# State-space stage of a two-layer decoder: a table of slots with an order of its own for each engine, and block-step rows in the decay matmul in place of the mask matmul

## The reference

```
xBCzA = input @ in_proj_w.T            # 1536 conv channels, 512 z, 64 heads of dt
xBC   = silu(causal_conv4(xBC) + bias) # x 512 (64 heads x 8), B and C 8 groups x 64
dt    = softplus(A_log);  dA = -dt
# in chunks of 128 tokens, s = query, z = key, for each of 64 heads:
Lm[s,z]    = exp(sum of dA over z < k <= s), 0 for z > s
Y_diag     = (C @ B.T * Lm) @ x
Y_off      = the state of the chunk before, decayed, through C
out        = ((Y_diag + Y_off + D * x / dt) * silu(z + z_bias)) @ out_proj_w.T
```

## Time and profile before

| | us |
|---|---|
| median of 3 timed runs | 995.61 (993.46 to 995.78) |
| the profiled execution | 996.49 |
| its span, first to last instruction | 994.6 |
| first decay slot of stage D to the last | 458.7 to 694.2 |
| TensorE, VectorE, ScalarE, GpSimd busy over the span | 807.5, 584.1, 381.4, 220.8 |
| granted TensorE clock, mean | 0.902 |

### The profile page before, as it was taken

How to read it: one execution, slowest core, us unless ns; L and a number is a source line. 1 busy time by engine, 2 the same in 40 slices (tenths; PEclk the granted TensorE clock), 3 DMA queues, 4 the chain that set the end, 5 groups by cost and what they waited for, 6 DMA issues and landing times.

```text
span 994.6 us, 14755 instructions
## 1 busy us (share of the span) xinstructions
PE 807.5 (81%) x5680; PEld 527.0 (53%) x5680; DVE 584.1 (59%) x1188; ACT 381.4 (38%) x653; POOL 220.8 (22%) x210
## 2 busy tenths in 40 slices
PE   1577777599799799656999898998667786899998
PEld 0334443258577578543444454343445464677776
DVE  5666642544445457635787888568567653545443
ACT  1124334101434345234455555454124344444442
POOL 4200000123442322141110111011311201432432
PEclk9889988799899899866899999699778788799999
DMA  8000001000121221000000000000000001222231
GB/s 311 28 2 1 3 1 49 1 0 21 57 70 62 65 63 33 9 0 5 5 4 5 4 4 6 3 5 4 1 2 2 1 2 50 75 85 64 82 95 41
DMA packets 17831, 32.77 MB, mean 33 GB/s; under 512 B 5819, under 2 KB 9787, under 8 KB 17494
## 3 DMA queue, kind: packets, MB, share of 16 engines
q1 hardware_dynamic: 17762, 31.83, 10.3%
HBM read 29.85 MB, written 1.05 MB: 31 GB/s over the span
## 4 chain that ended last, share of the span: by engine, by line
PE 60%; DVE 20%; issue 10%; ACT 5%; POOL 3%; DMA 1%; SPq 0%; DVEq 0%; ACTq 0%; POOLq 0%
PE bank L1355 13%; PE bank L1379 8%; PE bank L1394 5%; PE bank L1117 3%; PE bank L1455 3%; PE bank L1302 3%; PE bank L1453 3%; DVE s_xn L1526 2%; PE bank L1317 2%; DVE s_arena L1598 2%; PE bank L1246 2%; PE bank L1493 2%; PE bank L1400 2%; PE bank L1189 1%; POOL s_rstd L727 1%
## 5 line engine op out<-in xcount | busy, mean ns | idle before, releaser
L779 POOL TENSOR_TENSOR s_wl<-s_wmoe,s_wh 128x768 fp32r<-128x768 f32 x54 | 99.2, 1839 | 175.8 <-ACT s_wh L949 175.8
L898 ACT ACTIVATE s_arena<-bank 128x512 f32<-128x512 f32 x96 | 56.7, 597 | 107.3 <-PE bank L1222 56.8
L1717 DVE TENSOR_TENSOR s_act<-bank,s_sg_moe 128x512 f32<-128x512 f32 x54 | 37.3, 692 | 83.1 <-PE bank L1355 76.5
L1598 DVE TENSOR_REDUCE s_arena<-bank 128x2 f32<-128x512 f32 (+1 forms) x96 | 64.7, 687 | 34.0 <-PE bank L1193 17.3
L1355 PE MATMUL bank<-s_xh,s_wh 128*128 128x512 f32 x216 | 73.3, 422 | 9.0 <-POOL s_wl L779 9.0
L961 ACT CAST s_ah<-s_act 128x512 fp32r<-128x512 f32 x54 | 33.6, 621 | 102.6 <-DVE s_act L1722 79.3
L1355 PE MATMUL bank<-s_xl,s_wh 128*128 128x512 f32 x216 | 70.2, 408 | 0.0
L1379 PE MATMUL bank<-s_wh,s_ah 128*128 128x256 f32 x216 | 66.4, 308 | 2.8 <-DVE s_al L1728 2.8
L1355 PE MATMUL bank<-s_xh,s_wl 128*128 128x512 f32 x216 | 68.5, 399 | 0.0
L1752 DVE SCALAR_TENSOR_TENSOR s_arena<-s_arena,s_convw 128x256 f32<-128x256 f32 x144 | 67.9, 513 | 0.6
L1818 DVE TENSOR_TENSOR s_arena<-s_arena 128x512 f32<-128x512 f32 x64 | 43.4, 686 | 37.7 <-ACT s_arena L1058 37.5
(11 more groups left out here) (224 smaller groups left out, 1702.6 us busy)
## 6 DMA issues: line engine op xcount, KB each, us to landing
s_wmoe<-in_wF SPq DMA_DIRECT2D x28, 384.0 KB, 3.1
s_wmoe<-in_wC SPq DMA_DIRECT2D x26, 384.0 KB, 3.1
s_win<-in_win SPq DMA_DIRECT2D x1, 2112.0 KB, 10.4
s_x<-in_x SPq DMA_DIRECT2D x4, 256.0 KB, 3.4
s_early<-in_ctxT SPq DMA_DIRECT2D x1, 1024.0 KB, 9.5
s_ctxn<-in_ctx SPq DMA_DIRECT2D x1, 1024.0 KB, 12.2
s_arena<-s_arena SPq DMA_DIRECT2D x64, 6.0 KB
out_x<-s_x SPq DMA_DIRECT2D x4, 256.0 KB, 2.8
```

Of the source, the lines that this page charges most:

```text
L779: g.tensor_tensor(wl[:, w % NS_, :], wmoe[:, w % NW, :], wh[:, w % NS_, :], ALU.subtract).then_inc(wl_ready, 1)
L898: a.activation(PT[:, p % NPT, :], AR[n % 3][:, :], ACT.Exp).then_inc(a_read, 1)
L1598: v.tensor_reduce(nM[:, q, h0:h0 + heads], V[n % 2][:, :].rearrange("p (h k) -> p h k", h=heads), AX.X, ALU.max, negate=True).then_inc(v_r ...
```

## The change

1. `schedule` no longer puts all engines' parts in one step. `UNIT_SLOTS` and `PAIR_SLOTS` give for each kind its slot, with kinds of its own for TensorE (`dz`, `dz2`), ScalarE (`zth`) and VectorE (`zt`, `zsm`), and so on. The multiplication (`mul`) stands two slots after its decay matmul, the scan five as before, the exp at the end of its own slot. `din`, `dz` and `dy` are split in two halves in neighbouring slots. The first `cb` stands in slot 0 of unit 0.
2. The mask matmul goes. The decay matmul gets 15 more contraction rows (30 in all): for each border between blocks of 8 tokens, a row that is 1 for the keys of the block behind it (`blocks`) against a row that is -1e30 for queries before that block. Within a block of 8 the later keys are not masked there: `CBs` is multiplied with the lower triangle when it is copied, and the multiplication takes min(M, 1) first.
3. PSUM: decay matmuls alternate between two banks of their own (S), `din` in D and the x transpose share one (R), the B transpose goes to T.
4. One more DMA loads the block rows.

```diff
-LAST_UNIT = (5, "y_t"), (7, "dy_t"), (9, "dy")
-NEXT_UNIT = (6, "at"), (8, "dz"), (10, "zs"), (12, "xt"), (13, "cb")
-PAIR_AT = 1, 4, 9
 LAG = 5
-RR = 3 + 3 * HG
+MUL_LAG = 2
+UNIT_SLOTS = ((0, "cb", 0), (3, "state", 0), (3, "at", 1), (6, "y_t", -1), (7, "dz", 1), (8, "dz2", 1), (9, "dy_t", -1),
+              (12, "dy", -1), (13, "dy2", -1), (14, "xt", 1), (15, "xt1", 1),
+              (4, "atc", 1), (5, "ysc", -1), (7, "stc", 0), (10, "yfc", -1), (11, "zth", 1), (15, "xtc", 1), (15, "xtp", 1),
+              (16, "xt1c", 1),
+              (1, "cbc", 0), (4, "yo", 0), (7, "yfs", -1), (9, "zt", 1), (12, "zsm", 1), (14, "dx", -1))
+PAIR_SLOTS = (((1, "din"), (2, "din2"), (3, "ev"), (5, 1), (6, 2), (8, 3), (9, "th"), (10, "silu")),
+              ((4, "din"), (5, "din2"), (6, "ev"), (9, 1), (10, 2), (11, 3), (12, "th"), (13, "silu")),
+              ((10, "din"), (11, "din2"), (12, "ev"), (13, 1), (14, 2), (15, 3), (16, "th"), (18, "silu")))
+RL = 3 + 3 * HG
+STEPS = 16
+RR = RL + STEPS - 1
 GH = NHG // 2
...
-            chain = ["dt", "acum", "at", "ddt"]
+            chain = ["dt", "acum", "at", "atc", "ddt"]
...
-            if beside_c:
-                steps.append(("cb", s, 0))
...
+            slots = {}
+
+            def put(slot, kind, key):
+                slots.setdefault(slot, []).append((kind, s, key))
+
             for u in range(units + 1):
+                for p, kind, other in UNIT_SLOTS:
+                    v = u + other
+                    if not 0 <= v < units or (other == 1 and v == 0):
+                        continue
+                    if kind == "state" and v % 2 == 0:
+                        p += 3
+                    if (kind in ("stc", "xt1", "xt1c") and v % 2) or (kind == "yo" and v % 2 == 0):
+                        continue
+                    put(NHG * u + p, kind, v)
+                for n, marks in enumerate(PAIR_SLOTS):
+                    pair = divmod(FIRST_PAIRS + len(PAIR_SLOTS) * u + n, PAIRS)
+                    for p, kind in marks:
+                        if pair[0] < B:
+                            put(NHG * u + p, "tap" if kind in (1, 2, 3) else kind, (*pair, kind) if kind in (1, 2, 3) else pair)
+            for slot in range(NHG * (units + 1)):
+                u, p = divmod(slot, NHG)
+                if u < units:
+                    steps.append(("ssd", s, (u, p)))
+                if 0 <= slot - LAG < NHG * units:
+                    steps.append(("scan", s, divmod(slot - LAG, NHG)))
+                if 0 <= slot - MUL_LAG < NHG * units:
+                    steps.append(("mul", s, divmod(slot - MUL_LAG, NHG)))
+                steps.extend(slots.get(slot, []))
+                if u < units:
+                    steps.append(("exp", s, (u, p)))
...
-            fill("A" if ("switch", s, 0) in steps[:place] else "T", kind, s, *i)
+            fill("R" if ("switch", s, 0) in steps[:place] else "T", kind, s, *i)
...
+        S = bank[2:4]
+        R = bank[6]
...
+                    sp.dma_start(rows_z[RL:RR, :, :], A["blocks"]).then_inc(hot_in, 16)
...
-                            sp.wait_ge(a_full, at["A"]["ssd", s, i - 1, GH * (half + 1) - 1] + 1)
+                            sp.wait_ge(e_full, at["S"]["ssd", s, i - 1, GH * (half + 1) - 1] + 1)
...
+                    a.copy(Xt[:, i % 2, :], R[:, :]).then_inc(r_read, 1)
+                elif kind == "xt1c":
+                    act.wait_ge(t_full, at["T"]["xt1", s, i] + 1)
+                    if i:
+                        act.wait_ge(t_full, at["T"]["state", s, i - 2] + 1)
+                    a.copy(Bt, T[:, :]).then_inc(t_read, 1)
...
+                elif kind == "exp":
...
-                    a.activation(M[k % NM], AR[n % 3][:, :], ACT.Exp).then_inc(a_read, 1)
+                    a.activation(M[k % NM], S[k % 2][:, :], ACT.Exp).then_inc(e_read, 1)
...
+            def s_bank(*key):
+                n = at["S"][key]
+                if n >= 2:
+                    pe.wait_ge(e_read, n - 1)
+                return S[n % 2]
+
+            def r_bank(*key):
+                if at["R"][key]:
+                    pe.wait_ge(r_read, at["R"][key])
+                return R
...
-                    for h in range(2):
-                        ct = 2 * j + h
-                        for k in range(KD):
-                            ins = mm(bk[:, h * L:(h + 1) * L], win[:, k, ct * P:(ct + 1) * P],
-                                     xnT_of(s)[:, k, b * L:(b + 1) * L], start=(k == 0), stop=(k == KD - 1))
+                    for k in range(KD):
+                        mm(bk[:, 0:L], win[:, k, 2 * j * P:(2 * j + 1) * P],
+                           xnT_of(s)[:, k, b * L:(b + 1) * L], start=(k == 0), stop=(k == KD - 1))
+                elif kind == "din2":
+                    b, j = i
+                    bk, full = (T, t_full) if PAIRS * b + j < beside_c else (R, r_full)
+                    ct = 2 * j + 1
+                    for k in range(KD):
+                        ins = mm(bk[:, L:2 * L], win[:, k, ct * P:(ct + 1) * P],
+                                 xnT_of(s)[:, k, b * L:(b + 1) * L], start=(k == 0), stop=(k == KD - 1))
                     ins.then_inc(full, 1)
                 elif kind == "dz":
                     bk = v_bank("dz", s, i)
-                    for k in range(KD):
-                        ins = mm(bk[:, :], xnT_of(s)[:, k, i * P:(i + 1) * P], win[:, k, CONV:CONV + DI],
-                                 start=(k == 0), stop=(k == KD - 1))
-                    ins.then_inc(v_full, 1)
+                    mm(bk[:, :], xnT_of(s)[:, 0, i * P:(i + 1) * P], win[:, 0, CONV:CONV + DI],
+                       start=True, stop=False, skip_group_check=True)
+                elif kind == "dz2":
+                    mm(V[at["V"]["dz", s, i] % 2][:, :], xnT_of(s)[:, 1, i * P:(i + 1) * P], win[:, 1, CONV:CONV + DI],
+                       start=False, stop=True, skip_group_check=True).then_inc(v_full, 1)
...
-                    bk = a_bank("ssd", s, u, hg)
-
-                    mm(bk[:, :], identb[:, :], maskt[:, :].unsqueeze(1).to_broadcast([P, HG, P]),
-                       start=True, stop=False, skip_group_check=True)
-                    mm(bk[:, :], rows_z[:, hg, :], rows_s[:, :, hg, :], start=False, stop=True,
-                       skip_group_check=True).then_inc(a_full, 1)
-                    k = NHG * u + hg - LAG
-                    if k >= 0:
-                        scan(s, *divmod(k, NHG))
-                elif kind == "ssd_end":
-                    for k in range(NHG * i - LAG, NHG * i):
-                        scan(s, *divmod(k, NHG))
+                    bk = s_bank("ssd", s, u, hg)
+
+                    mm(bk[:, :], rows_z[:, hg, :], rows_s[:, :, hg, :], start=True, stop=True
+                       ).then_inc(e_full, 1)
+                elif kind == "scan":
+                    scan(s, *i)
...
-                    for k in range(DI // P):
-                        ins = mm(bk[:, 0:D], yfT[:, k, :], wout[:, k, :], start=(k == 0), stop=(k == DI // P - 1))
+                    for k in range(DI // P // 2):
+                        mm(bk[:, 0:D], yfT[:, k, :], wout[:, k, :], start=(k == 0), stop=False, skip_group_check=True)
+                elif kind == "dy2":
+                    for k in range(DI // P // 2, DI // P):
...
+                    if i >= 1:
+                        dve.wait_ge(zs_ready, i)
...
-                elif kind == "cb":
+                elif kind == "cbc":
                     for par in range(2):
                         n = at["V"]["cb", s, i, par]
                         dve.wait_ge(v_full, n + 1)
-                        v.tensor_copy(CBs[:, i % 2, par:NG:2, :], V[n % 2][:, :].rearrange("p (g s) -> p g s", g=NG // 2)
-                                      ).then_inc(v_read, 1)
-                elif kind == "ssd":
+                        v.scalar_tensor_tensor(CBs[:, i % 2, par:NG:2, :],
+                                               V[n % 2][:, :].rearrange("p (g s) -> p g s", g=NG // 2), -1.0,
+                                               tri[:, 0, :].unsqueeze(1).to_broadcast([P, NG // 2, P]),
+                                               ALU.mult, ALU.mult).then_inc(v_read, 1)
+                elif kind == "mul":
                     u, hg = i
                     if hg == 0:
 
                         dve.wait_ge(v_read, at["V"]["cb", s, u, 1] + 1)
 
-                    dve.wait_ge(a_read, at["A"]["ssd", s, u, hg] + 1)
+                    dve.wait_ge(e_read, NHG * u + hg + 1)
                     m = M[(NHG * u + hg) % NM].rearrange("p (h z) -> p h z", h=HG)
-                    v.tensor_tensor(m, m, CBs[:, u % 2, hg // (NV // NG):NG:NG // HG, :], ALU.mult).then_inc(m_ready, 1)
+                    v.scalar_tensor_tensor(m, m, 1.0, CBs[:, u % 2, hg // (NV // NG):NG:NG // HG, :], ALU.min, ALU.mult
+                                           ).then_inc(m_ready, 1)
...
```

(51 more changed lines are left out.)

60 lines of the change are left out of this document (26 added, 34 removed).

## The result

The changed kernel takes 1019.05 us (median of 4 runs, 1017.51 to 1019.30), the kernel before 995.69 us: ratio 1.0217 (95% interval 1.0195 to 1.0239). It is slower by 2.2%, where 959 us was forecast. The profiled execution took 1019.15 us, its span is 1017.3 us and TensorE's mean granted clock 0.833, where it was 0.902.

What follows compares the result with a forecast made beforehand. TensorE was taken as the bound, VectorE next and taking over in units 1 to 4 after the change. Unit savings of 2.7 + 17.8 + 8.9 + 4.6 + 2.5 = 36.5 us from 996.5, less 0.9, gave 959 us; range 944 to 984.

Steps and rivals of the forecast that it cites:

- The depth costs nothing: Mask matmul removed, 0.31 us a slot, 40 us of TensorE; the 30-row decay matmul takes no longer, to within 2 ns.
- The three-operand forms: VectorE's multiplication with a min and C·B copy: 0 us added, bounds 0 to 6 us.
- The places: Own slots per engine, projections halved: no slot over about 1.2 us beside its own work, VectorE's idle lumps gone.
- friction of 9%: Allowance on the larger of VectorE's and TensorE's work in units 1 to 4, giving 113.3 us, was 131.1.
- TensorE's floor: Least unit time on TensorE: its earlier busy time less 5.0 us; 23.3 us in unit 2.
- The bank waits: New PSUM banks for decay matmuls and projections: TensorE may stand 0.5 us, twice a unit at most, counted in friction.
- rival B: Engines in lockstep through ScalarE's waits for VectorE's taps and too few banks: friction 20%, 981 us; chance 0.14.
- The C·B product in slot 0: First C·B product moved from start-up into unit 0: +1.1 us TensorE, +1.3 us VectorE.
- The sum: Unit by unit, the larger of VectorE's and TensorE's work plus friction: 36.5 us saved over the eight units.
- term of unit 7: Last unit, ending on VectorE's work for the next stage's head: 18.2 us, was 20.7.
- Rival C: Slow clock in units 1 to 4 as well as 5 to 7, slower than before: 1010 us; chance 0.07.
- Rival A: Slow clock in units 5 to 7, where no projection wakes it: 984 us all slow, 972 likely; chance 0.14.

Runs made afterwards that it cites:

- 128-row kernel: The changed kernel with its decay matmul 128 contraction rows deep in place of 30, the added rows zero on both sides: 963.02 us, ratio 0.9625.

## Why the prediction was wrong, by its own steps

1. The mask matmul. The 0.31 us a slot went, and the deeper decay matmul costs no time at full clock: 0.31 us from its start (541.58) to the scan's (541.89) in unit 2 (rows under 3). "The depth costs nothing" was right for duration. The reading stopped there: what depth does for the clock was put at nothing, without a reason.
2. The three-operand forms: 0 us was taken, and 691 to 693 and 683 ns were measured. Right.
3. The places. Right, and undersized: with projections the full-clock unit is 25.14 us where 27.6 was taken. The friction of 9% was not there in units 2 and 4: TensorE is busy 25.14 of 25.14 us. It, and not VectorE (21.5 and 22.8), is the bound there with 30 rows; with 128 rows both are busy 23.9 of 24.7 us. TensorE's floor was put too low, though: its busy time in unit 2 fell by 3.2 us (28.34 to 25.14), not by 5.0. Halving the projections costs it time, a term that the prediction put at nothing: two halves take 2.13 us (1.06 and 1.07, from their start to the next decay matmul's), a whole one 1.73 (542.17 to 543.90 in the earlier trace rows).

```profile
538.78 1.13 PE L1414 MATMUL bank<-s_xnT,s_win 128*128 128x256 f32 x4
539.84 0.38 PE L1485 MATMUL bank<-s_arena 30*128 30x512 bf16 x1
...
540.51 1.13 PE L1421 MATMUL bank<-s_xnT,s_win 128*128 128x256 f32 x4
541.58 0.38 PE L1485 MATMUL bank<-s_arena 30*128 30x512 bf16 x1
541.89 0.43 PE L1139 MATMUL bank<-s_early,s_wmoe 128*32 128x128 f32 x8
```

4. The bank waits. TensorE stood for one exp 2.10 us, not 0.5, at the end of unit 0, behind tanh, a tap and an eviction: rival B's chain, in one place. The eviction's wait for VectorE in units 1 and 3 was missed altogether. Step 4 costed the new banks and not the old semaphore, which the new places put on the wrong side of VectorE's state work.
5. and 6. The C·B product in slot 0 and the DMAs: unit 0 started at 457.7 us where it was 458.7. Its price was taken at full clock (1.1 us); it was 2.0 us at the half clock, as unit 0 starts slow.

The step that failed is in "The sum": the units were costed at the clock they had before, unit 5 even at a better one ("half of its slow stretch gone"), while the mask matmul that this clock hung on was taken out. The measured stage is 261.2 us, at a mean clock of 0.66, where the sum gives 199. The 128-row kernel is the check: with the clock near that of before (0.91 in the stage, 0.93 before), the same order and the same work, its stage is 202.2 us and its time 963 us, against 199 and 959 forecast. So 59 of the 62 us went with the depth, as clock and as weight loads that start earlier. In units 2 and 4, where both kernels are at 1.00, they differ by 0.4 us each, so nearly all of it is the clock.

That 202 comes so near to 199 is in part luck. Units 2 and 4 of the 128-row kernel are 2.9 us each under their terms (27.6), and units 0, 3 and 7 are 2.0, 2.4 and 4.6 over theirs. The term of unit 7, 18.2 us, is also below the prediction's own floor for it, 18.3, and has no friction.

Rival C was the outcome and had 0.07. It named the mechanism, put units 5 to 7 at 87 us when all slow (94.7 measured) and two units with projections at 41 each (46.9 and 37.6 for 1 and 3), 1010 us in all. Rival A named it for units 5 to 7 alone, and its sign, a clock under 0.8 there, came (0.59, 0.50, 0.50). What spoke against C was misread: that units 6 and 7 ran at 1.00 "with bare slots", and that projections brought the clock back in units 1 and 3 within about 5 us (it was 6.8 and 3.4). Both were seen with the mask matmul in every slot, the very thing that went. The earlier trace rows were a warning that the mask alone does not bring the clock back: the stretch there lasted 17 us with the mask in the slots, and it is absent where the decay matmul beside it is 128 rows deep too.

On the Trainium skill's rule ("TensorE: Matmul & The Clock Gate", section "A second HAM failure mode: psum-queue depth-cycling"): the swinging came, and after short waits. But the 128-row kernel cycles through the same two banks with a wait of 2.40 us in the same place, and its clock in that unit and the next is 0.83 and 0.94, not 0.66 and 0.52. The number of slow stretches does not follow the banks either: in the profiled runs with 128 rows and no mask, the new order with its two banks has seven in the stage, the old order with its ring of three has eight. A short wait comes before the falls looked at above (not every such wait has one behind it: units 2 and 4 of the earlier trace rows); how long the clock then stays down depends on the depth and, in the one run that shows it, on a further wait.

## What to carry to other kernels

Before a matmul is taken out, or replaced by a shallow one, look at what it is for the clock: evidence that a stretch stays at full clock holds only for the mix of matmuls in it. If a frequent matmul has few contraction rows, try padding it with zero rows: it cost no time at full clock here, it raised the mean clock of the stage from 0.66 to 0.91, and it turned +2.2% into -3.8%. A short full-depth matmul in front of it did not do the same. When each engine gets its own order, check every old semaphore against the new places, above all a wait for a later engine's work that stands in for an earlier engine's read.

## What the runs showed of the hardware

- TensorE's clock held better the deeper the decay matmul's contraction was, at equal columns and instructions: stage 261, 221 and 202 us, mean clock in it 0.66, 0.83 and 0.91, with 30, 64 and 128 rows; whether the added rows of the moving side hold zeros or ones makes no difference (963.0 and 962.9 us).
- Depth is not all: with a full-depth mask matmul in every slot beside the 30-row one, the clock was still at 0.50 for 20.5 us in unit 7, and what the order is worth changes sign with the depth (12.5 us lost in the stage with 30 rows, 13.6 gained with 128).
- At 1.2 GHz the clock can stay for whole units although TensorE is busy without a gap (units 6 and 7 after: 59 us at 0.50).
- Behind the mask matmul, the weight load for a matmul of 128 rows starts while the mask still runs; the one for 15 rows does not: 0.23 against 0.31 us from start to start.
